# A graph network of four layers: gathers begun three places ahead instead of two, and the maximum's pieces at the front of a place

## The chip, the core and the metric

The kernel runs on one core of one Trainium2 chip. The metric is the time of the whole program on the device, in microseconds. The engines are PE (TensorE: matmuls and transposes), DVE (VectorE), ACT (ScalarE), POOL (GpSimd) and SP (SyncE, which here only issues DMAs); each runs its own instructions in order and waits for the others by semaphores.

## What is computed

Eight graphs (batches) of 2048 nodes with 256 features go through four layers; each layer adds its output to x. The adjacency is 0/1 and symmetric.

```python
h = relu(layernorm(x)); x = x + L0(adj, h)   # the first 25 neighbours' features, elementwise maximum
h = relu(layernorm(x)); x = x + L1(h, adj)   # attention, 4 heads of 64
h = relu(layernorm(x)); x = x + L2(h, adj)   # mean over the neighbours
h = relu(layernorm(x)); x = x + L3(h, adj)   # attention, one head of 256

# L0, for every node:
vals, idx = top_k(where(A != 0, -arange(N), -inf), 25)
agg = max over the 25 rows h[idx]            # rows that don't exist: -inf, or 0 where degree <= 25
out = relu(concatenate([h, agg]) @ W + b)
```

## The kernel before

A tile is 128 nodes; a batch has 16 tiles, the program 128. Layer 0 of batch b+1 is worked beside layers 1 to 3 of batch b, and that of batch 0 by itself at the start (the opening). Its work on one tile is cut in two halves. The **front** of a tile (`slot_front`) loads its adjacency rows, casts them on ACT, transposes them on PE, evacuates them on ACT (kept for the later layers in `adjT`), packs eight bits to a word on PE, and lets DVE find the first 25 neighbours; their numbers go to `idx`, which has two buffers. POOL then issues 25 indirect DMAs, each of which gathers one neighbour's row (256 f32) for the 128 nodes into `gath`, also two buffers of 25 rows. The **back** of a tile (`slot_back`) waits for the gather, takes the maximum of the 25 rows into `cat` (DVE), transposes the concatenation (PE), copies it (ACT), multiplies by W (PE) and adds to x (DVE).

A place (slot) is the back of tile T and the front of tile T + LAG, in 16 parts. `slot` calls each engine's work part by part: PE's transposes of the adjacency at parts 0 and 5 and its packing at 3 and 8; ACT's evacuations at 1, 2, 6, 7 and the copy of the adjacency word at 9 (L655); DVE's selection at 12 to 15 (it begins with `key`, L1120, and ends with `idx`, L1143); the concatenation's transposes at 10, ACT's copy at 11 (L677), the product at 12, DVE's addition at 15 (L1184). DVE's maximum is done in four pieces at the parts of `MAX_AT`. In the opening (`alone`) a piece is one reduction of a quarter of the columns (L1161); later the pieces are pairwise maxima of halves (L1152) and a last one into `cat` (L1178), which signals `reduced`.

`body` lays the parts of the places between the steps of the main work of a batch, evenly over a pair of steps' blocks. `PLAN` says how many places each phase takes: prep1 2, attend1 (four heads) 4, prep2 2, mean 3, prep3 1, attend3 (one head) 4. The first eight places of the opening, and one or two places in the phases prep1 to prep3, also carry `pre`, which normalises and stores the next batch's h in the table that the gathers read. Since every engine is in order, a part that waits holds up all the main work behind it on that engine.

POOL's work is `slot_front` alone, at part 15: it waits for `reduced.free(T, 2)`, that is for the maximum of tile T − 2, whose `gath` buffer it fills, and for `idx_ready`. `table_row`, `pre` and SP's loads of `cat` and `x1` stay as they are.

Of the kernel before, what the change touches and what calls it, by code (L numbers as in the profile page):

```python
# [48 lines left out]
S = 25  # L49
# [7 lines left out]
LAG = 2  # L57
# [47 lines left out]
def gnn_kernel(nc, x, adj, w0, b0, w1, a1s, a1d, w2m, w2u, b2, w3, a3, const, out):  # L105
    ctx = ExitStack()
    with ctx:
# [182 lines left out]
        MAX_AT = (0, 3, 6, 8)  # L290
# [6 lines left out]
        def body(eng, b, do, front=lambda s: True, pre=True, slots=True):  # L297
# [86 lines left out]
        def program(eng, do):  # L384
# [27 lines left out]
        class Part:  # L412
# [8 lines left out]
            def slot_back(self, T, par, n, part, front, alone): pass  # L421
# [17 lines left out]
            def slot(self, b, sh, par, part, front, k):  # L439

                known = isinstance(sh, int)
                alone = isinstance(b, int) and b < 0
                enters = not known or front(2 * sh + par)
                next_enters = not known or front(2 * sh + par + 1)
                Tf, Tb, n = front_tile(b, sh, par), back_tile(b, sh, par), half(b, sh)
                if part == 0:  # L450
                    self.slot_back(Tb, par, n, part, enters, alone)
                if enters:
                    self.slot_front(Tf, par, n + LAG // 2, part)
                if k is not None:
                    self.pre(16 * (b + 2) + 2 * k, 8 * (b + 2) + k, part)
                if part != 0:
                    self.slot_back(Tb, par, n, part, enters, alone)
                if next_enters:
                    self.ahead(Tf + 1, part)
# [24 lines left out]
        def _(sp):  # L484
            class Do(Part):
# [54 lines left out]
                def slot_back(self, T, par, n, part, front, alone):  # L540
# [64 lines left out]
        def _(act):  # L605
            class Do(Part):
# [66 lines left out]
                def slot_back(self, T, par, n, part, front, alone):  # L673
# [135 lines left out]
        def _(pe):  # L809
            class Do(Part):  # L810
# [41 lines left out]
                def slot_back(self, T, par, n, part, front, alone):  # L852
# [142 lines left out]
        def _(dve):  # L995
# [57 lines left out]
            class Do(Part):  # L1053
# [63 lines left out]
                def slot_front(self, T, par, n, part):  # L1117
# [32 lines left out]
                def slot_back(self, T, par, n, part, front, alone):  # L1150
# [5 lines left out]
                    if alone and part in MAX_AT:  # L1156
                        i = MAX_AT.index(part)
# [7 lines left out]
                    if part == MAX_AT[0]:  # L1165
                        halve(0, 12, 6)
                    if part == MAX_AT[1]:
                        halve(6, 18, 6)
                    if part == MAX_AT[2]:
# [3 lines left out]
                    if part == MAX_AT[3]:  # L1173
# [5 lines left out]
                    if part in MAX_AT:  # L1179
# [175 lines left out]
```

## Time and profile before

| | us |
|---|---|
| time before, median of 3 runs | 7518.04 (7516.22 to 7602.97) |
| the profiled execution's own time | 7535.86 |
| its span in the trace | 7534.0 |
| PE, DVE, ACT, POOL busy | 5252.3, 4670.5, 2088.6, 3479.3 |

The program has three stretches: the opening up to about 740 us, seven batches of some 900 us each with layer 0 of the next batch beside them, and the last batch from about 7000 us by itself. A row of the timeline gives the start and the length of an instruction, its line, the tiles out<-in, and in brackets how long its engine was idle before it and who released it; "remote" is a release for which the trace has no origin, "issue" a rest in which the engine waited for nothing that the trace shows. Matmuls are named by their accumulator.

### The profile page before, as it was taken

What the parts mean: (1) busy time and instruction counts of PE and PEld (TensorE: products, weight loads), DVE (VectorE), ACT (ScalarE), POOL (GpSimd) and SP (SyncE); (2) the same over time, 40 slices, a digit from 0 to 9 for tenths busy, and PEclk for the clock granted to TensorE, in tenths of its full rate; (3) what the DMA queues carried; (4) which work ended last, traced back from release to release, by engine and by line L of the source; (5) the groups of instructions that cost most, each with busy time, mean ns of one, the idle gap of its engine ahead of it and who ended that gap; (6) DMA issues with size and microseconds to landing.
All of it is one profiled execution on the core that took longest, in us unless ns stands there. A gap on an engine that the chain in (4) does not pass through costs nothing.

```text
span 7534.0 us, 85178 instructions
## 1 busy us (share of the span) xinstructions
PE 5252.3 (70%) x23860; PEld 3104.4 (41%) x23860; DVE 4670.5 (62%) x9897; ACT 2088.6 (28%) x4103; POOL 3479.3 (46%) x3204
## 2 busy tenths in 40 slices
PE   1212786778867696676866769667786669767999
PEld 1111334553345432463335533355334543356347
DVE  5544685457745587456865569546785458745653
ACT  2211323322233222323133131332323322231222
POOL 4656445454444544555444544446445454554000
PEclk8555897888878798887988889788898879878999
DMA  5434226442263423633245322544226442363021
GB/s 161 136 114 121 86 71 184 121 122 77 85 183 115 126 63 103 193 115 100 65 131 167 111 87 76 156 141 134 80 78 185 119 124 76 101 184 90 6 71 53
DMA packets 660564, 849.36 MB, mean 113 GB/s; under 512 B 80356, under 2 KB 491752, under 8 KB 659944
## 3 DMA queue, kind: packets, MB, share of 16 engines
q0 software_dynamic: 153600, 419.64, 19.2%
q10 hardware_dynamic: 344064, 268.50, 12.5%
q1 hardware_dynamic: 162408, 155.53, 6.5%
q8 instruction: 204, 3.34, 0.2%
q14 instruction: 288, 2.36, 0.1%
HBM read 774.13 MB, written 69.21 MB: 112 GB/s over the span
## 4 chain that ended last, share of the span: by engine, by line
PE 43%; another core or an unknown queue 19%; DVE 15%; issue 12%; ACT 5%; DMA 3%; ACTq 2%; DVEq 1%; SPq 0%
PE acc L951 17%; PE acc L957 8%; PE acc L897 4%; DVE edge L1264 4%; DVE top L1047 3%; DVE key L1050 2%; PE acc L987 2%; PE acc L989 2%; PE acc L988 2%; PE psH L864 2%; ACT hb L686 1%; DVE gath L1152 1%; PE psT L833 1%; PE psB L918 1%
## 5 line engine op out<-in xcount | busy, mean ns | idle before, releaser
L597 POOL DMA_INDIRECT gath<-htab,idx x3200 | 3479.1, 1087 | 3449.4 <-issue 1960.6
L951 PE MATMUL acc<-edge,region 128*65 128x512 f32 x4096 | 1861.3, 604 | 113.9 <-DVE edge L1264 86.6
L1264 DVE SCALAR_TENSOR_TENSOR edge<-region,gg,adjT 128x1024 f32<-128x1024 f32 (+1 forms) x1536 | 1640.8, 1107 | 351.5 <-ACT region L739 107.1
L957 PE MATMUL acc<-region,edge 128*128 128x257 f32 x4096 | 1018.6, 402 | 174.6 <-issue 92.7
L951 PEld LDWEIGHTS acc<-edge,region 128*65 128x65 f32 x4096 | 550.7, 140 | 1161.1 <-issue 1011.4
L957 PEld LDWEIGHTS acc<-region,edge 128*128 128x128 f32 x4096 | 804.8, 201 | 327.4 <-issue 167.1
L1152 DVE TENSOR_TENSOR gath<-gath 128x1536 f32<-128x1536 f32 (+2 forms) x672 | 782.6, 1178 | 55.0 <-issue 20.4
L639 ACT ACTIVATE adjT_b<-psT 128x1024 bf16<-128x1024 bf16 x256 | 262.7, 1026 | 1452.7 <-PE psT L833 689.6
L897 PE MATMUL acc<-w_s,edge 128*128 128x512 f32 (+2 forms) x1536 | 625.2, 554 | 3.8 <-issue 3.8
L1047 DVE MAX8 top<-key 128x8 f32<-128x256 f32 (+1 forms) x1024 | 407.3, 398 | 156.4 <-remote 48.2
L1120 DVE SCALAR_TENSOR_TENSOR key<-psO,cst 128x256 f32<-128x256 f32 x128 | 54.0, 422 | 722.8 <-ACT cst L655 603.4
L987 PE MATMUL acc<-region,col_b 128*128 128x257 bf16 x1024 | 297.0, 290 | 146.4 <-issue 79.7
L897 PEld LDWEIGHTS acc<-w_s,edge 128*128 128x128 f32 x1536 | 339.1, 236 | 138.7 <-issue 91.6
L1318 DVE TENSOR_SCALAR den<-acc 128x1 f32<-128x1 f32 x128 | 20.0, 156 | 587.5 <-remote 307.3
L987 PE MATMUL acc<-region,edge 128*128 128x257 bf16 x1024 | 299.3, 292 | 92.0 <-ACT edge L793 66.2
L864 PE MATMUL psH<-w_s,catT 128*128 128x256 f32 x1024 | 341.6, 491 | 0.0
L874 PE MATMUL psB<-cst,hb 128*128 128x128 f32 x768 | 150.2, 329 | 270.1 <-ACT hb L686 169.1
L833 PE MATMUL psT<-ident_bf,adj_b 128*128 128x128 bf16 x2048 | 203.1, 242 | 192.6 <-ACT adj_b L660 108.7
L988 PE MATMUL acc<-region,col_b 128*128 128x256 bf16 x1024 | 297.0, 290 | 36.2 <-issue 35.9
L989 PE MATMUL acc<-region,edge 128*128 128x256 bf16 x1024 | 299.2, 292 | 23.4 <-issue 23.0
L988 PE MATMUL acc<-region,edge 128*128 128x256 bf16 x1024 | 298.5, 291 | 22.4 <-issue 22.3
L989 PE MATMUL acc<-region,col_b 128*128 128x256 bf16 x1024 | 298.7, 292 | 20.8 <-issue 20.4
(130 smaller groups left out, 5897.3 us busy)
## 6 DMA issues: line engine op xcount, KB each, us to landing
adj_i<-in_adj ACTq DMA_DIRECT2D x512, 256.0 KB
hb<-in_adj ACTq DMA_DIRECT2D x256, 256.0 KB
col_i<-in_adj ACTq DMA_DIRECT2D x256, 256.0 KB
gath<-htab,idx POOLq DMA_INDIRECT x3200
cat<-htab SPq DMA_DIRECT2D x128, 128.0 KB
x<-in_x SPq DMA_DIRECT2D x128, 128.0 KB
x1d<-x SPq DMA_DIRECT2D x128, 128.0 KB
xr<-x1d SPq DMA_DIRECT2D x32, 512.0 KB
```

The lines of the kernel that those rows point to most:

```text
L597: pool.indirect_dma_start(out=gath[:, par, s, :], out_offset=None, in_=htab, in_offset=bass.IndirectOffsetOnAxis(ap=idx[:, par, s:s + 1], ...
L833: ins = pe.transpose(psT[:, 512 * k + P * j:512 * k + P * j + P], adj_b[:, k, P * j:P * j + P], ident_bf[:, :])
L864: ins = pe.matmul(o_mm, catT[:, k, :], w0_s[:, k, :], start=False, stop=(k == 3))
L897: ins = pe.matmul(bank[:, 0:width], hT[n % 2][:, i, c, :], w[:, c, :], start=(c == 0), stop=(c == 1 and p != 2), skip_group_check=True)
L951: ins = pe.matmul(acc[0:F + 1, 2 * h + half, :], V[1][:, J, (F + 1) * head:(F + 1) * (head + 1)], here[:, 512 * half:512 * half + 512], st ...
L957: ins = pe.matmul(acc[:, k, 0:C + 1], here[:, P * k:P * k + P], V[3][:, J, :], start=(J == 0), stop=(J == NT - 1), skip_group_check=True)
L987: pe.matmul(acc[:, k, 0:C + 1], w, split[:, t, 2 * C:3 * C + 1], start=(t == 0), stop=False, skip_group_check=True)
L988: pe.matmul(acc[:, k, 0:C], w, split[:, t, 0:C], start=False, stop=False, skip_group_check=True)
L989: ins = pe.matmul(acc[:, k, 0:C], w, split[:, t, C:2 * C], start=False, stop=(t == NT - 1), skip_group_check=True)
L1047: steps.of(dve.max(top[:, 8 * r:8 * r + 8], values))
L1152: steps.of(dve.tensor_tensor(gath[:, par, a:a + n, :], gath[:, par, a:a + n, :], gath[:, par, b:b + n, :], ALU.max))
L1264: dve.scalar_tensor_tensor(ring[p][:, n % EDGES[p], :], wB_of[p][:, h if p == 1 else q, :], gg[:, J, head:head + 1], adjT[:, J, bass.ds((( ...
```

## The change

LAG goes from 2 to 3. The front in a place is now that of tile T + 3; since 3 is odd it goes to the other `idx` and `gath` buffer than the tile whose back stands in the same place. The prologue ahead of the loop makes three fronts instead of two, and the last batch but one has one front fewer. The two-deep `gath` stays, so POOL's gather for tile T + 3 waits for the maximum of T + 1. As the indices of T + 3 overwrite those of T + 1, DVE waits for the gather of T + 1 before it writes them. The pieces of the maximum stand at parts 0, 1, 2, 3 in the opening and in all phases but attend1, where they stay at 0, 3, 6, 8.

```diff
-LAG = 2
+LAG = 3
...
-        MAX_AT = (0, 3, 6, 8)
+        MAX_AT = {True: (0, 3, 6, 8), False: (0, 1, 2, 3)}
...
                     k = pre_0 + i if pre and i < pres else None
-                    side += [lambda part=part, sh=sh, par=par, k=k: do.slot(b, sh, par, part, front, k) for part in range(PARTS)]
+                    apart = phase == "attend1"
+                    side += [lambda part=part, sh=sh, par=par, k=k: do.slot(b, sh, par, part, front, k, apart) for part in range(PARTS)]
...
             for T in range(LAG):
                 for part in range(PARTS):
-                    do.slot_front(T, T, 0, part)
+                    do.slot_front(T, T % 2, T // 2, part)
...
                 if enters:
-                    self.slot_front(Tf, par, n + LAG // 2, part)
+                    self.slot_front(Tf, (LAG + par) % 2, n + (LAG + par) // 2, part)
...
                     if part == 15:
                         first_bits(key[:, 0:S * WORD], 1, 4)
 
+                        if not isinstance(T, int) or T >= 2:
+                            dve.wait_ge(gathered[par], 16 * S * n)
                         dve.tensor_scalar(idx[:, par, :], top[:, 0:S], -1.0, cst[:, bass.ds(T + C_OFF, 1)], ALU.mult, ALU.add)\
...
+                    max_at = MAX_AT[apart]
...
-                    if part == MAX_AT[0]:
+                    if part == max_at[0]:
                         halve(0, 12, 6)
```

Three places in the order of the instructions, which shifts by one to four line numbers after the change.

POOL at the start of the program, up to its loop over the opening's places (`x24` is the rest of a tile's gathers). Before:

```order
L597 DMA gath<-htab,idx 128x256 [waits idx_ready,h_dma,reduced]
L597 DMA gath<-htab,idx 128x256 x24
L597 DMA gath<-htab,idx 128x256 [waits idx_ready,h_dma,reduced]
L597 DMA gath<-htab,idx 128x256 x24
L399 UNCONDITIONAL_BRANCH
L593 ISA [waits h_dma]
L597 DMA gath<-htab,idx 128x256 [waits reduced,idx_ready]
L597 DMA gath<-htab,idx 128x256 x24
L593 REGISTER_ALU [waits h_dma]
```

After:

```order
L598 DMA gath<-htab,idx 128x256 [waits idx_ready,h_dma,reduced]
L598 DMA gath<-htab,idx 128x256 x24
L598 DMA gath<-htab,idx 128x256 [waits idx_ready,h_dma,reduced]
L598 DMA gath<-htab,idx 128x256 x24
L598 DMA gath<-htab,idx 128x256 [waits idx_ready,h_dma,reduced]
L598 DMA gath<-htab,idx 128x256 x24
L400 UNCONDITIONAL_BRANCH
L594 ISA [waits h_dma]
L598 DMA gath<-htab,idx 128x256 [waits reduced,idx_ready]
```

A third tile's 25 gathers now stand ahead of the loop.

DVE in the opening, from the end of one place's selection to the next place's maximum. Before:

```order
L1047 MAX top<-key 128x8 [waits chain]
L1143 ISA [waits chain]
L1143 TENSOR_SCALAR idx<-top,cst 128x25
L1015 ISA [waits idx_ready,chain]
L1182 REGISTER_ALU
L1184 SCALAR_TENSOR_TENSOR x<-psH,x 128x256 [waits x1_ld,o_done]
L1161 TENSOR_REDUCE cat<-gath 128x64 [waits cat_tr,gathered1]
L1161 TENSOR_REDUCE cat<-gath 128x64 x3
```

After (`gathered1` is the buffer of the tile whose maximum follows):

```order
L1048 MAX top<-key 128x8 [waits chain]
L1145 ISA [waits chain]
L1146 ISA [waits gathered1]
L1146 TENSOR_SCALAR idx<-top,cst 128x25
L1016 ISA [waits idx_ready,chain]
L1186 REGISTER_ALU
L1188 SCALAR_TENSOR_TENSOR x<-psH,x 128x256 [waits x1_ld,o_done]
L1165 TENSOR_REDUCE cat<-gath 128x64 [waits cat_tr,gathered1]
L1165 TENSOR_REDUCE cat<-gath 128x64 x3
```

The wait for the gather now also stands ahead of the indices.

DVE in attend3, the second of its four places, from the third to the last piece of the maximum (L1264, after the change L1268, makes an attention edge). Before:

```order
L1152 TENSOR_TENSOR gath<-gath 128x1536
L1152 TENSOR_TENSOR gath<-gath 128x768 [waits chain]
L1015 ISA [waits chain]
L1261 REGISTER_ALU
L1264 REGISTER_ALU [waits mm3]
L1264 SCALAR_TENSOR_TENSOR edge<-region,gg,adjT 128x512
L1261 REGISTER_ALU
L1264 REGISTER_ALU [waits mm3]
L1264 SCALAR_TENSOR_TENSOR edge<-region,gg,adjT 128x512
L1152 TENSOR_TENSOR gath<-gath 128x256 x2
L1178 TENSOR_TENSOR cat<-gath 128x256 [waits cat_tr,chain]
L1015 ISA [waits chain]
```

After:

```order
L1155 TENSOR_TENSOR gath<-gath 128x1536
L1155 TENSOR_TENSOR gath<-gath 128x768 [waits chain]
L1016 ISA [waits chain]
L1265 REGISTER_ALU
L1268 REGISTER_ALU [waits mm3]
L1268 SCALAR_TENSOR_TENSOR edge<-region,gg,adjT 128x512
L1155 TENSOR_TENSOR gath<-gath 128x256 x2
L1182 TENSOR_TENSOR cat<-gath 128x256 [waits cat_tr,chain]
L1016 ISA [waits chain]
L1265 REGISTER_ALU
```

Between the third and the fourth piece there were two edges, now there is one.

## Rows read from the trace of the kernel before

**Rows 1.** The page: span, busy time of each engine, a group of instructions
```profile
span 7534.0 us, 85178 instructions
PE 5252.3 (70%) x23860; PEld 3104.4 (41%) x23860; DVE 4670.5 (62%) x9897; ACT 2088.6 (28%) x4103; POOL 3479.3 (46%) x3204
...
L1152 DVE TENSOR_TENSOR gath<-gath 128x1536 f32<-128x1536 f32 (+2 forms) x672 | 782.6, 1178 | 55.0 <-issue 20.4
```

**Rows 2.** The tile of the gathered rows: durations (ns), who waited for it (us, times)
```profile
L597 POOL DMA_INDIRECT gath<-htab,idx x3200: 941/949/2561, 43.7 to 6928.0; - x189
...
  DVE cat L1161: 36.9, 5
```

**Rows 3.** Stretches: opening; batch 5's attend1, mean, attend3; last batch's mean, attend3
```profile
core 0: us, PE busy (x) PEld busy (x) DVE busy (x) ACT busy (x) POOL busy (x), PEclk, DMA share, GB/s
77.00:722.00 645.00, 125.70 (x711) 85.79 (x711) 334.41 (x647) 115.94 (x172) 377.97 (x399) 0.57 0.42 122
5336.60:5601.10 264.50, 249.75 (x782) 90.43 (x783) 230.20 (x316) 58.78 (x134) 113.01 (x94) 0.98 0.23 68
5714.70:5883.90 169.20, 113.57 (x895) 86.80 (x896) 82.93 (x251) 62.81 (x103) 76.61 (x74) 0.82 0.69 203
5946.70:6127.00 180.30, 143.12 (x708) 117.01 (x709) 116.03 (x247) 36.69 (x61) 116.75 (x105) 0.90 0.43 126
7294.80:7385.40 90.60, 88.16 (x766) 75.87 (x767) 26.75 (x96) 41.64 (x67) 0.00 (x0) 0.94 0.72 207
7411.00:7528.40 117.40, 114.69 (x524) 99.21 (x524) 49.50 (x78) 7.12 (x17) 0.00 (x0) 0.98 0.04 14
```

**Rows 4.** Waits (engine line <- whom: us, times, longest): opening, then 740 to 7534
```profile
ACT adjT_b L639 <- remote: 376.4, 16, 34.8
...
DVE key L1120 <- ACT cst L655: 459.8, 31, 29.0
```

**Rows 5.** Timeline of the opening, POOL then ACT: start, us, what [idle before <-releaser]
```profile
121.30 0.95 POOL L597 DMA_INDIRECT gath<-htab,idx  x1 [14.95 <-issue]
...
353.36 0.95 POOL L597 DMA_INDIRECT gath<-htab,idx  x1 [7.70 <-issue]
...
392.01 0.94 POOL L597 DMA_INDIRECT gath<-htab,idx  x1 [7.63 <-issue]
...
474.73 0.95 POOL L597 DMA_INDIRECT gath<-htab,idx  x1 [20.43 <-issue]
...
388.65 1.02 ACT L639 ACTIVATE adjT_b<-psT 128x1024 bf16<-128x1024 bf16 x1 [18.47 <-remote]
...
434.29 1.02 ACT L639 ACTIVATE adjT_b<-psT 128x1024 bf16<-128x1024 bf16 x1 [28.29 <-remote]
...
462.32 1.02 ACT L639 ACTIVATE adjT_b<-psT 128x1024 bf16<-128x1024 bf16 x1 [25.05 <-remote]
```

**Rows 6.** Timeline of the opening, DVE
```profile
77.07 11.02 DVE L1161 TENSOR_REDUCE cat<-gath 128x64 f32<-128x1600 f32 x4 [14.43 <-DMA gath<-htab,idx]
...
367.99 0.42 DVE L1120 SCALAR_TENSOR_TENSOR key<-psO,cst 128x256 f32<-128x256 f32 x1
...
390.97 0.24 DVE L1143 TENSOR_SCALAR idx<-top,cst 128x25 uint32<-128x25 f32 x1 [0.16 <-DVE top L1047]
...
464.56 0.42 DVE L1120 SCALAR_TENSOR_TENSOR key<-psO,cst 128x256 f32<-128x256 f32 x1 [28.75 <-ACT cst L655]
...
473.69 0.24 DVE L1143 TENSOR_SCALAR idx<-top,cst 128x25 uint32<-128x25 f32 x1 [0.15 <-DVE top L1047]
```

**Rows 7.** Timeline of batch 0's mean phase: POOL, PE, ACT
```profile
1226.80 0.94 POOL L597 DMA_INDIRECT gath<-htab,idx  x1 [0.30 <-issue]
...
1218.34 0.26 PE L833 MATMUL psT<-ident_bf,adj_b 128*128 128x128 bf16 x1 [1.13 <-issue]
...
1231.28 1.02 ACT L639 ACTIVATE adjT_b<-psT 128x1024 bf16<-128x1024 bf16 x1 [16.46 <-remote]
```

**Rows 8.** Timeline of batch 3's attend3 phase: POOL, ACT
```profile
4341.51 0.95 POOL L597 DMA_INDIRECT gath<-htab,idx  x1 [51.42 <-DVE idx L1143]
...
4295.66 0.60 ACT L677 ACTIVATE catT<-psH 128x512 f32<-128x512 f32 x1 [50.85 <-remote]
```

More of the change, by code:

```diff
@@ L420, in slot_front, with slot_back @@
             def slot_front(self, T, par, n, part): pass
-            def slot_back(self, T, par, n, part, front, alone): pass
+            def slot_back(self, T, par, n, part, apart, alone): pass
             def prep_start(self, p, b): pass
@@ L437, in end, with slot @@
             def end(self, b): pass
-            def slot(self, b, sh, par, part, front, k):
+            def slot(self, b, sh, par, part, front, k, apart=False):
                 known = isinstance(sh, int)
@@ L450, in slot @@
                 if part == 0:
-                    self.slot_back(Tb, par, n, part, enters, alone)
+                    self.slot_back(Tb, par, n, part, apart, alone)
                 if enters:
-                    self.slot_front(Tf, par, n + LAG // 2, part)
+                    self.slot_front(Tf, (LAG + par) % 2, n + (LAG + par) // 2, part)
                 if k is not None:
@@ L456, in slot @@
                 if part != 0:
-                    self.slot_back(Tb, par, n, part, enters, alone)
+                    self.slot_back(Tb, par, n, part, apart, alone)
                 if next_enters:
@@ L538, in pre, with slot_back @@
                             sp.dma_start(htab[bass.ds(table_row(u + i), P), :], xa[:, i, :]).then_inc(h_dma, 16)
-                def slot_back(self, T, par, n, part, front, alone):
+                def slot_back(self, T, par, n, part, apart, alone):
                     if part == 0:
@@ L671, in ahead, with slot_back @@
                         self.cast(T, part - 14)
-                def slot_back(self, T, par, n, part, front, alone):
+                def slot_back(self, T, par, n, part, apart, alone):
                     if part == 11:
@@ L850, in slot_front, with slot_back @@
                         pack((3, 8).index(part))
-                def slot_back(self, T, par, n, part, front, alone):
+                def slot_back(self, T, par, n, part, apart, alone):
                     if part == 10:
@@ L1148, in slot_front, with slot_back @@
                         steps.end()
-                def slot_back(self, T, par, n, part, front, alone):
+                def slot_back(self, T, par, n, part, apart, alone):
                     def halve(a, b, n):
                         steps.of(dve.tensor_tensor(gath[:, par, a:a + n, :], gath[:, par, a:a + n, :], gath[:, par, b:b + n, :], ALU.max))
+                    max_at = MAX_AT[apart]
                     if part == 0:
                         dve.wait_ge(gathered[par], 16 * S * n + 16 * S)
-                    if alone and part in MAX_AT:
-                        i = MAX_AT.index(part)
+                    if alone and part in max_at:
+                        i = max_at.index(part)
                         if i == 0:
@@ L1164, in slot_back @@
                         return
-                    if part == MAX_AT[0]:
+                    if part == max_at[0]:
                         halve(0, 12, 6)
-                    if part == MAX_AT[1]:
+                    if part == max_at[1]:
                         halve(6, 18, 6)
-                    if part == MAX_AT[2]:
+                    if part == max_at[2]:
                         halve(0, 6, 6)
@@ L1172, in slot_back @@
                         halve(0, 3, 3)
-                    if part == MAX_AT[3]:
+                    if part == max_at[3]:
                         halve(0, 2, 1)
@@ L1178, in slot_back @@
                         dve.tensor_tensor(cat[:, C:2 * C], gath[:, par, 0, :], gath[:, par, 1, :], ALU.max).then_inc(reduced.sem, 1)
-                    if part in MAX_AT:
+                    if part in max_at:
                         steps.end()
```

## The prediction

> **What bounds the kernel now.** I read the page first, then the gather's tile, a table of stretches, the waits, and the timelines of the opening, of one mean phase and of the worst stall.
>
> No engine is full: PE is busy 5252 us of 7534, DVE 4671, POOL 3479 [rows 1]. The gathers are 3200 indirect DMAs, 25 for each of 128 tiles. Almost nobody waits for them: DVE waited 36.9 us in 5 places of the opening [rows 2], and all the idle time in front of the later maxima is 55.0 us [rows 1]. So a gather that lands earlier is worth at most 36.9 + 55.0 = 92 us by itself.
>
> What matters more is what happens beside a gather. In the opening (16 places, 77 to 722 us) PE works 126 us of 645 and DVE 334 [rows 3]; the greatest wait is ACT's for PE's transposes, 376.4 us in 16 pieces, which the trace puts down to nobody ("remote") [rows 4]. The timelines show its shape. A gather starts at 353.36 and ends 7.63 us before 392.01, at 384.38, so it takes 31.0 us. ACT's evacuation comes at 388.65, after 18.47 us of waiting that began some 17 us into that gather [rows 5]. DVE needs from 367.99 to 390.97, 23.0 us, for a chain of selections that takes 464.56 to 473.69, 9.1 us, while POOL rests [rows 6]. From 392.01 on two gathers stand back to back and end at 474.73 − 20.43 = 454.3; ACT waits 28.29 us and again 25.05 us, until 462.32, 8 us behind the last [rows 5]. In the mean phase a single gather does it: PE's transposes, a tenth of a microsecond apart by themselves, come with rests of 1.13 us, and ACT is let go at 1231.28, some 3.5 us after POOL's last issue of 1226.80 ended [rows 7]. So I read: the first 16 or so of a gather's 31 us cost the others nothing, the rest and 3 to 8 us behind it slow every engine's small instructions and signals (the loud end, below), and back-to-back gathers are the worst case. What causes it the trace doesn't tell. Long instructions don't mind it: four reductions keep their 11.0 us [rows 6].
>
> How much of that lies in the later batches: compare batch 5 with the last one, which has no places. Mean: PE busy 113.6 of 169.2, against 88.2 of 90.6. One-head attention (attend3): 143.1 of 180.3, against 114.7 of 117.4. PE idles 55.6 + 37.2 = 92.8 us in the two where the last batch idles 5.1; seven batches make 614 us that are neither PE's old nor its new work. The four-head attention leaves less: 249.8 of 264.5 [rows 3].
>
> **The change part by part.** *One more front ahead of the loop.* The prologue now selects tile 2 too. Part of it falls on DVE's 14.43 us of waiting for gather 0 [rows 6]; in exchange the last batch but one has one front fewer, and I set the rest equal to that. But gather 2, which now starts at 121.30 after 14.95 us of rest [rows 5], can follow gather 1 at once: −15 us.
>
> *The gather of tile T+3 waits for the maximum of T+1, no longer for a selection just finished.* Its indices are ready a place before, so it starts when the maximum at the front of the next place is done. In the opening the quiet first 16 us of a gather then cover the concatenation, the statistics and the fast selection; its loud end falls on the next 11.0 us of reduction, which don't mind. A place of the first eight takes 392.01 − 353.36 = 38.7 us [rows 5]: 11.0 of reduction, 23.0 of selection, 1 for the result, 3.7 left for the statistics. With the selection at 9.1 it would be 24.8, and POOL would bind at 25 × 1.25 = 31.3: up to 7.4 us each, 59 for eight. But with POOL bound its gathers stand back to back, the bad case, so I take under half: −25 us. The last eight take (645 − 8 × 38.7) / 8 = 41.9 us each. There I see a cycle of two gathers back to back, 62.6 us, and then a rest until the result and one reduction are through, 3 + 11 us: 77 for two, 38.5 each, 3.4 less, 27 for eight, of which I take −20 us.
>
> *The later batches.* A place is 40 to 80 us long (180.3 / 4 = 45 in the one-head attention [rows 3]) and a gather 31 and more of them, so POOL keeps up either way, and the same number of gathers falls in each phase. What moves is which parts of the place the loud end meets. Before, the gather starts with the place and its end meets parts 5 to 9, where PE and ACT hand the adjacency back and forth, with PE's attention matmuls queued behind on PE. After, it starts behind part 3 (part 8 in the four-head attention) and its end meets parts 10 to 15: three handovers (concatenation, copy, result) and DVE's selection. DVE's wait for the adjacency word, 459.8 us in 31 pieces behind the opening [rows 4], is the one that becomes shorter. It isn't all on the path, since in attention eight edge buffers lie between DVE and PE. Bounds: 0, and the whole 614 of PE's idle time. I take a tenth of the 460, −46 us, near zero because the gathers' number and length stay the same.
>
> *The maximum's pieces at parts 0 to 3 rather than 0, 3, 6, 8.* The same operations, 782.6 us for 112 tiles, 7.0 us each [rows 1], now nearly in one go. In the one-head attention eight edges lie in store, by the last batch 8 × 117.4 / 64 = 14.7 us of PE work [rows 3]: hidden; were it not, 7 us a place would cost 7 × 28 = 196. In the mean DVE owes only short finishes, each up to 7 us later with four accumulators: hidden. In the four-head attention, where DVE is busy 230 of 264 us [rows 3], nothing moves. 0 us.
>
> *The new wait ahead of the indices* asks for gather T+1 at part 15, just ahead of the wait that was there at part 0 of the next place. Queued behind it on DVE are the indices and the result's addition. It costs only where a place is shorter than POOL's 31.3 us: the opening, counted above. 0 us elsewhere.
>
> Sum: 7534 − 15 − 25 − 20 − 46 = 7428 for the profiled execution, whose own time of 7536 is 18 above the median of 7518. So **7410 us**.
>
> A rule bears on this. The Trainium skill, "DMA: Bandwidth & Descriptors", Rules for kernel authors, says to issue a DMA early, do other work, and wait for its semaphore late. By that rule alone the gain is at most what is waited for on gathers now, and the rows say that little is left of it; it would give 7426 on the median at best.
>
> **The rivals.** *The quiet start is worth more (7280).* If the opening comes near POOL's bound (645 down to 16 × 31.3 + 44 = 545, −100) and a fifth of the 614 is saved (−123), the sum with the −15 is 7534 − 238 = 7296, about 7280 on the median. For it: DVE's chain of 23.0 against 9.1 us [rows 6]. Against it: back-to-back gathers [rows 5].
>
> *Nothing changes (7510).* Gathers weren't waited for, their number is the same, and the loud end only meets other instructions. For it: PE crawls in the mean whatever stands in its queue [rows 7].
>
> *Slower (7620).* The result's chain meets the loud end. Now that is seen at one place: gathers without rest until 4341.51 − 51.42 = 4290.1, and ACT's copy of the concatenation waits 50.85 us until 4295.66, with PE and DVE's result behind it [rows 8]. After the change parts 10 to 12 always stand some 20 us into a gather. If each result must wait for the gather's end and 5 us more, a place can't be shorter than about 10 + 35 + 5 = 50 us; in the one-head attention it is 45 now, so 5 us times 28 places, 140 us, less the opening's 35: 7639, on the median about 7620. It decides from the point where gather end + 5 lies behind part 15.
>
> A further rule: the Trainium skill, "GPSIMD Engine Reference", section 8, says that GpSimd shares its SBUF interfaces with VectorE, with contention when VectorE reads two SBUF inputs. The trace agrees: one issue takes 378.0 / 399 = 0.95 us in the opening and 113.0 / 94 = 1.20 us in the four-head attention [rows 3]. It changes POOL's time only, which has rest to spare there.
>
> **How the numbers follow.** Forecast (7330 to 7480) 0.44, large gain 0.20, nothing 0.18, slower 0.18. The likeliest gives 7410. The range, 7280 to 7590, leaves out about half of the large gain and half of the slower case. Two per cent, about what can be told from no change, lies at 7368 and 7668: faster is the large gain and a quarter of the forecast, 0.31; slower is the part of its case in which more than the one-head attention pays, 0.13; the rest is 0.56.
>
> **What would show it.** In the profile after: gather 2 at about 107 us; the opening's places at 33 to 40 us; gathers starting 1 us behind the maximum, at the front of a place; ACT's nameless waits for transposes in the opening well below 376 us; DVE's wait for the adjacency word under 460. Wrong would be: mean or one-head attention longer than 170 and 180 us with ACT waiting for the concatenation until a gather ends, or more gathers back to back.

## The result, and the profile after

| | us |
|---|---|
| time after, median of 4 runs | 8379.53 (8366.68 to 8414.74) |
| time before, on the same chip, median of 4 runs | 7529.19 (7516.22 to 7602.97) |
| ratio | 1.111, 95% interval 1.103 to 1.120 |

The change makes the kernel 11% slower. I had forecast 7410 us and a range up to 7590; even the rival that ended on the slow side, 7620, is 760 us short. The page of the kernel after, with its most telling groups (busy us, mean ns | idle us of the engine just before them, and what ended it):

```profile
span 8412.9 us, 85400 instructions
...
PE 5272.2 (63%) x23860; PEld 3099.1 (37%) x23860; DVE 4670.1 (56%) x9897; ACT 2083.4 (25%) x4103; POOL 3161.8 (38%) x3204
...
L598 POOL DMA_INDIRECT gath<-htab,idx x3200 | 3161.6, 988 | 4606.5 <-DVE cat L1182 3344.1
...
L1155 DVE TENSOR_TENSOR gath<-gath 128x1536 f32<-128x1536 f32 (+2 forms) x672 | 781.9, 1177 | 45.8 <-issue 7.4
...
L1121 DVE SCALAR_TENSOR_TENSOR key<-psO,cst 128x256 f32<-128x256 f32 x128 | 54.0, 422 | 926.7 <-issue 546.1
```

The work is the same as in [rows 1]: PE 5272 busy us against 5252, DVE 4670 against 4671, and the maxima take 781.9 against 782.6. POOL is even 317 us less busy. The span is 879 us longer, nearly all of it waiting. POOL's idle time ahead of a gather is now put down to DVE's last piece of the maximum, 3344 us of it. The gathers, whose effect on the others was my whole argument, are now the ones who wait.

The stretches that answer to [rows 3] (opening; attend1, mean and attend3 of batch 5; the columns are those of [rows 3]):

```profile
core 0: us, PE busy (x) PEld busy (x) DVE busy (x) ACT busy (x) POOL busy (x), PEclk, DMA share, GB/s
77.00:818.00 741.00, 124.30 (x744) 84.84 (x744) 344.00 (x675) 121.68 (x181) 399.80 (x421) 0.57 0.38 111
6010.50:6290.50 280.00, 256.53 (x783) 91.99 (x783) 230.06 (x316) 59.28 (x135) 93.65 (x85) 0.95 0.20 59
6433.70:6632.80 199.10, 116.50 (x896) 90.45 (x897) 83.01 (x251) 62.10 (x103) 71.11 (x75) 0.77 0.59 173
6694.60:6917.40 222.80, 152.93 (x707) 121.05 (x708) 115.73 (x247) 36.62 (x60) 98.39 (x100) 0.81 0.33 99
```

The opening is 741 us against 645, attend1 280.0 against 264.5, mean 199.1 against 169.2, attend3 222.8 against 180.3, with the busy time of DVE and ACT unchanged. Everything that carries a place is longer, attend3 most; the last batch, which has none, takes 557 us against 556 before, from the first matmul of its main work to the last. PE's granted clock is lower (mean 0.834 before, 0.798 after, between its levels of 1.2 and 2.4 GHz), but all PE busy time has grown by 20 us only: the clock is no cause here.

**One place of attend3, before.** POOL's first issue of two gathers, then DVE, then ACT (start, us, [idle before <- releaser]):

```profile
1484.62 0.95 POOL L597 DMA_INDIRECT gath<-htab,idx  x1 [16.33 <-issue]
...
1534.57 1.48 POOL L597 DMA_INDIRECT gath<-htab,idx  x1 [14.59 <-issue]
...
1485.38 1.75 DVE L1152 TENSOR_TENSOR gath<-gath 128x1536 f32<-128x1536 f32 x1
...
1499.74 0.42 DVE L1178 TENSOR_TENSOR cat<-gath 128x256 f32<-128x256 f32 x1
...
1521.94 0.42 DVE L1120 SCALAR_TENSOR_TENSOR key<-psO,cst 128x256 f32<-128x256 f32 x1 [19.06 <-issue]
...
1533.53 0.24 DVE L1143 TENSOR_SCALAR idx<-top,cst 128x25 uint32<-128x25 f32 x1 [0.15 <-DVE top L1047]
1534.14 0.42 DVE L1184 SCALAR_TENSOR_TENSOR x<-psH,x 128x256 f32<-128x256 f32 x1 [0.36 <-DVEq L1010]
...
1521.52 0.38 ACT L655 ACTIVATE cst<-psO 128x256 f32<-128x256 f32 x1 [18.45 <-remote]
```

The gather starts at 1484.62 and its last issue ends 14.59 us before 1534.57, at 1519.98: 35.4 us. The whole maximum, 1485.38 to 1500.16, lies beside its first half. Then DVE waits 19.06 us for the adjacency word, which ACT copies at 1521.52, 1.5 us behind the gather. Behind that stand only the selection (to 1533.77) and the next gather's start. Place: 35.4 + 14.6 = 50 us.

**One place of attend3, after:**

```profile
1640.31 1.31 POOL L598 DMA_INDIRECT gath<-htab,idx  x1 [25.84 <-DVE cat L1182]
...
1695.48 1.31 POOL L598 DMA_INDIRECT gath<-htab,idx  x1 [23.39 <-DVE cat L1182]
...
1639.06 0.42 DVE L1182 TENSOR_TENSOR cat<-gath 128x256 f32<-128x256 f32 x1
...
1666.39 0.42 DVE L1121 SCALAR_TENSOR_TENSOR key<-psO,cst 128x256 f32<-128x256 f32 x1 [20.94 <-issue]
...
1678.35 0.24 DVE L1146 TENSOR_SCALAR idx<-top,cst 128x25 uint32<-128x25 f32 x1 [0.15 <-DVE top L1048]
1682.06 0.42 DVE L1188 SCALAR_TENSOR_TENSOR x<-psH,x 128x256 f32<-128x256 f32 x1 [3.48 <-PE psH L865]
...
1683.25 1.75 DVE L1155 TENSOR_TENSOR gath<-gath 128x1536 f32<-128x1536 f32 x1
...
1694.22 0.42 DVE L1182 TENSOR_TENSOR cat<-gath 128x256 f32<-128x256 f32 x1
...
1665.97 0.38 ACT L656 ACTIVATE cst<-psO 128x256 f32<-128x256 f32 x1 [13.77 <-remote]
...
1676.04 0.60 ACT L678 ACTIVATE catT<-psH 128x512 f32<-128x512 f32 x1 [8.89 <-remote]
```

The gather runs from 1640.31 to 1695.48 − 23.39 = 1672.09, 31.8 us, and nothing large lies beside it: DVE waits 20.94 us ahead of the key, ACT 13.77 ahead of the word and 8.89 ahead of the concatenation. The result comes at 1682.06, 10 us behind the gather, and only then does the next maximum run, 1683.25 to 1694.64, and the next gather starts behind its last piece. Place: 31.8 + 11.2 + 12.2 = 55.2 us. The gather that starts there had its indices since 1678.59, and the rows that this maximum reads had been issued by 1640.31 − 25.84 = 1614.47. It isn't data that is late. The maximum has moved from beside the gather to between two gathers.

Over all gathers of the seven attend3 phases (25 of each kernel; worked out from the trace; a gather is counted to the end of its last issue): before, a gather 34.4 us and 11.8 us from its end to the next one, 46.2 in all; after, 31.9 + 25.3 = 57.2. In the mean phases 33.6 + 24.4 = 58.0 before, 31.1 + 36.3 = 67.4 after. That POOL needs 317 us less is the same fact: an issue is slower beside DVE's maximum, and none is beside it now.

**The opening, after:**

```profile
124.44 0.95 POOL L598 DMA_INDIRECT gath<-htab,idx  x1 [21.86 <-DVE cat L1165]
...
401.16 0.95 POOL L598 DMA_INDIRECT gath<-htab,idx  x1 [29.88 <-DVE cat L1165]
...
493.21 0.95 POOL L598 DMA_INDIRECT gath<-htab,idx  x1 [29.72 <-DVE cat L1165]
...
101.10 0.42 DVE L1121 SCALAR_TENSOR_TENSOR key<-psO,cst 128x256 f32<-128x256 f32 x1 [42.18 <-issue]
...
112.56 11.09 DVE L1165 TENSOR_REDUCE cat<-gath 128x64 f32<-128x1600 f32 x4 [0.54 <-DVEq L1011]
...
415.32 11.01 DVE L1165 TENSOR_REDUCE cat<-gath 128x64 f32<-128x1600 f32 x4
...
471.01 0.42 DVE L1121 SCALAR_TENSOR_TENSOR key<-psO,cst 128x256 f32<-128x256 f32 x1 [27.49 <-ACT cst L656]
...
481.35 11.03 DVE L1165 TENSOR_REDUCE cat<-gath 128x64 f32<-128x1600 f32 x4
...
454.57 1.02 ACT L640 ACTIVATE adjT_b<-psT 128x1024 bf16<-128x1024 bf16 x1 [41.86 <-remote]
```

Two gathers from 401.16 stand back to back until 493.21 − 29.72 = 463.49; ACT waits 41.86 us in them for transposes, DVE gets its key at 471.01, and then come selection, result and maximum in a row before POOL may go on: 493.21 − 401.16 = 92.05 us for two places. And the first maximum is taken at 112.56, not at 77.07 [rows 6], since DVE stands 42.18 us at the key of the third front.

### The profile page after: what moved, and what is told of

Read it like the earlier page. It is cut to its first block, busy times and chain, and to the rows that moved or that the text cites. A ratio compares the mean times of both kernels' runs of the same rounds, so it can differ in the third digit from the quotient of the medians.

```text
span 8412.9 us, 85400 instructions
## 1 busy us (share of the span) xinstructions
PE 5272.2 (63%) x23860; PEld 3099.1 (37%) x23860; DVE 4670.1 (56%) x9897; ACT 2083.4 (25%) x4103; POOL 3161.8 (38%) x3204
## 3 DMA queue, kind: packets, MB, share of 16 engines
q10 hardware_dynamic: 344064, 268.50, 11.2%
## 4 chain that ended last, share of the span: by engine, by line
PE 36%; another core or an unknown queue 23%; issue 17%; DVE 15%; ACT 5%; DMA 2%; ACTq 2%; DVEq 1%; SPq 0%
PE acc L952 12%; PE acc L958 6%; DVE edge L1268 5%; PE acc L898 4%; DVE gath L1155 3%; PE acc L988 3%; PE acc L990 2%; PE acc L989 2%; DVE top L1048 2%; DVE key L1051 2%; PE psH L865 1%; DMA col_i<-in_adj 1%; PE psB L919 1%; PE psB L875 1%
## 5 line engine op out<-in xcount | busy, mean ns | idle before, releaser
L598 POOL DMA_INDIRECT gath<-htab,idx x3200 | 3161.6, 988 | 4606.5 <-DVE cat L1182 3344.1
L952 PE MATMUL acc<-edge,region 128*65 128x512 f32 x4096 | 1882.9, 609 | 136.2 <-DVE edge L1268 70.5
L1268 DVE SCALAR_TENSOR_TENSOR edge<-region,gg,adjT 128x1024 f32<-128x1024 f32 (+1 forms) x1536 | 1635.5, 1104 | 457.1 <-ACT region L740 154.5
L958 PE MATMUL acc<-region,edge 128*128 128x257 f32 x4096 | 1067.4, 411 | 343.8 <-issue 251.3
L958 PEld LDWEIGHTS acc<-region,edge 128*128 128x128 f32 x4096 | 821.9, 205 | 525.5 <-issue 328.6
L1155 DVE TENSOR_TENSOR gath<-gath 128x1536 f32<-128x1536 f32 (+2 forms) x672 | 781.9, 1177 | 45.8 <-issue 7.4
L898 PE MATMUL acc<-w_s,edge 128*128 128x512 f32 (+2 forms) x1536 | 580.7, 520 | 109.3 <-ACT edge L694 109.2
L898 PEld LDWEIGHTS acc<-w_s,edge 128*128 128x128 f32 x1536 | 312.8, 218 | 233.8 <-ACT edge L694 110.6
L844 PE MATMUL psO<-pack_bf,adjT_b 128*128 128x32 bf16 x2048 | 105.3, 180 | 468.2 <-issue 360.1
L863 PE MATMUL psH<-bias 3*128 3x256 bf16 x128 | 42.3, 331 | 464.4 <-ACT catT L678 306.7
```

What stands on the lines that cost most here:

```text
L598: pool.indirect_dma_start(out=gath[:, par, s, :], out_offset=None, in_=htab, in_offset=bass.IndirectOffsetOnAxis(ap=idx[:, par, s:s + 1], ...
L898: ins = pe.matmul(bank[:, 0:width], hT[n % 2][:, i, c, :], w[:, c, :], start=(c == 0), stop=(c == 1 and p != 2), skip_group_check=True)
L952: ins = pe.matmul(acc[0:F + 1, 2 * h + half, :], V[1][:, J, (F + 1) * head:(F + 1) * (head + 1)], here[:, 512 * half:512 * half + 512], st ...
L958: ins = pe.matmul(acc[:, k, 0:C + 1], here[:, P * k:P * k + P], V[3][:, J, :], start=(J == 0), stop=(J == NT - 1), skip_group_check=True)
L1268: dve.scalar_tensor_tensor(ring[p][:, n % EDGES[p], :], wB_of[p][:, h if p == 1 else q, :], gg[:, J, head:head + 1], adjT[:, J, bass.ds((( ...
```

## The experiments

**Which half of the change is it?** The pieces at the front alone, and the three places alone.

```diff
-LAG = 3                          # lag2_front_max; and without the wait ahead of the indices
+LAG = 2
```
```diff
-        MAX_AT = {True: (0, 3, 6, 8), False: (0, 1, 2, 3)}        # lag3_old_max
+        MAX_AT = {True: (0, 3, 6, 8), False: (0, 3, 6, 8)}
```

> Only the pieces of the maximum move to parts 0 to 3 outside attend1; gathers stay two places ahead. Theory L (the loop): in the changed kernel a gather can start only behind the maximum of the next place, that maximum stands on DVE behind the last place's result, and the result is held until the running gather has ended, so a place costs gather + result + maximum in a row. With LAG 2 a gather starts on its indices, so nothing of that arises: 7450 to 7600 us. Rival B (the burst): four pieces in a row hold up DVE's edges and finishes, 7 us in 96 later places and more: 8000 us or more.

Measured: 7613 us, ratio 1.013 (1.009 to 1.017): 13 us above the range of theory L, far from B's 8000.

> LAG 3 with the pieces at parts 0, 3, 6, 8 everywhere. Theory L: the gather starts later in its place still, so it is as slow as the changed kernel or slower, 8400 to 9200 us. Rival B: the loss is undone, 7500 to 7600 us.

Measured: 8411 us, ratio 1.119 (1.113 to 1.124): as L has it, and B falls. The pieces cost 1.3% by themselves, mostly in attend3 (a phase has 196 us against 184), where I had set 0 us. The rest is the three places; with them, the old positions of the pieces inside a place make nothing better.

**Is it the order, or just POOL's wait?** The kernel before with one digit changed: a gather waits for the maximum of the tile ahead of its own, as it does with three places and two buffers.

```diff
-                    pool.wait_ge(reduced.sem, reduced.free(T, 2))
+                    pool.wait_ge(reduced.sem, reduced.free(T, 1))
```

> The kernel before, but POOL waits for the maximum of tile T-1 instead of T-2 ahead of the gather of T, so that the gather starts behind the next place's maximum as in the changed kernel; LAG, indices and the order on every other engine are as before. Theory L: gather and maximum come one after the other and the gather must land within its own place: 8400 us or more. Rival D (the third tile in flight and the new wait ahead of the indices are what costs): about 7530, at most 7700 us.

Measured: 8443 us, ratio 1.123 (1.117 to 1.128).

```profile
L597 POOL DMA_INDIRECT gath<-htab,idx x3200 | 3142.7, 982 | 4699.9 <-DVE cat L1178 3327.0 <-issue 1120.7 <-DVE cat L1161 208.9
...
L1152 DVE TENSOR_TENSOR gath<-gath 128x1536 f32<-128x1536 f32 (+2 forms) x672 | 781.5, 1177 | 275.8 <-DMA gath<-htab,idx 222.4 <-DVEq L1010 15.4 <-issue 11.4
...
DVE cat L1161 <- DMA gath<-htab,idx: 284.2, 14, 23.9
```

Nearly the same loss and the same signature (4700 us of idle POOL, 3327 of it for DVE's last piece) with LAG, selection and result as before; theory L holds, D falls. The match of the totals is in part chance, since a gather must now land within its own place: DVE waits 222 us for rows behind the opening and 284 in it, which the changed kernel does not. The clean part is the mean and attend3 phases, where hardly any rows are waited for (19 us in all): they take 195.5 and 216.8 us on average of the seven batches, against 197.2 and 221.0 after the change and 172.0 and 184.5 before, and in attend3 a gather of 31.5 us is followed by 25.2. There the loss sits in one relation: a gather that may start only behind the maximum that DVE takes next.

**Does the late result hold the maximum?** After the change DVE's result stands between the gather's end and the maximum. Moved earlier, outside attend1, it should let the maximum go sooner.

```diff
-                    if part == 10:      # PE, concatenation; ACT's copy 11 -> 5, product 12 -> 6, DVE's result 15 -> 10
+                    if part == (10 if apart else 4):
```

> The changed kernel with the result outside attend1 moved ahead: the concatenation's transposes at part 4, its copy at 5, the product at 6, DVE's addition at 10, that is into the first 16 us of the gather that the maximum releases. Theory L, with the result as the step that is held: the result comes before the gather's loud end and the next maximum stands only behind the selection, 7700 to 8200 us. If it is the selection (the adjacency word) that is held as long as the result, no change: 8300 to 8450. Rival B: no change.

Measured: 8785 us, ratio 1.168 (1.162 to 1.174): slower still, and outside all three expectations.

```profile
L1188 DVE SCALAR_TENSOR_TENSOR x<-psH,x 128x256 f32<-128x256 f32 x128 | 54.3, 424 | 634.3 <-remote 469.6 <-PE psH L865 75.9 <-issue 75.5
L1121 DVE SCALAR_TENSOR_TENSOR key<-psO,cst 128x256 f32<-128x256 f32 x128 | 53.8, 421 | 1004.1 <-ACT cst L656 765.6 <-issue 231.7 <-DVEq L1011 6.3
```

DVE's idle time ahead of the key went from 927 to 1004 us and ahead of the result from 217 to 634. The key now starts 4 us behind the gather's end (median of the places from tile 20 on; after the change 17 us ahead of it, with the result 8 us behind it), and the whole selection stands between it and the maximum. In attend3 a gather of 31.6 us is followed by 30.4 us, against 25.3. Moving one handover earlier doesn't free the path; it decides which one is held, and how much is queued behind it.

**Does it go if the maximum is taken out of the loop?** With three places DVE can take tile T+1's maximum in the place of T, ahead of the selection, so that the gather starts behind the indices again.

```diff
-        MAX_AT = {True: (0, 3, 6, 8), False: (0, 1, 2, 3)}
+        MAX_AT = {True: (2, 5, 8, 11), False: (8, 9, 10, 11)}
...
+                    T, n, par = T + 1, n + par, 1 - par     # in DVE's slot_back, for the maximum only
```

> LAG 3 as in the changed kernel, but DVE takes the maximum of tile T+1 at parts 8 to 11 of place T (2, 5, 8, 11 in attend1), ahead of that place's selection and result, so that the gather of T+3 can start as soon as its indices are written; tile 0's maximum stands ahead of the loop. Theory L: with the maximum out of the way between one gather and the next the loss is gone, 7400 to 7650 us, though LAG is 3, three fronts stand ahead and the new wait is there. Rival D (the third tile in flight, the other buffer, the new wait): stays above 8200.

Measured: 7966 us, ratio 1.064 (1.058 to 1.071), between the two theories. attend3 is back at 185 us a phase (35.0 + 13.2 a gather), but the mean phase has 188 and the opening is still 85 us longer than before. DVE now waited 576 us ahead of the last piece, and 235 more ahead of the opening's reductions; both overwrite the concatenation that PE transposes at part 10: a wait the experiment had brought along. Two more kernels were to take it away: result at parts 4 to 7 (lag3_ahead_early), and the pieces besides at 0, 3, 6, 8 outside the opening (lag3_ahead_front).

> Three places ahead, the maximum of tile T+1 taken in the place of T at parts 8 to 11 as in the run before with that change (7965 us), and now also the result of T earlier in every place: PE's transposes of the concatenation at part 4, ACT's copy at 5, the product at 6, DVE's addition at 7. In that earlier run DVE waited 576 us ahead of the last piece of the maximum, which overwrites the concatenation that PE transposes only at part 10; the two lie side by side. Theory W (that wait, which the experiment itself put in, is the rest of the loss): with the transposes at part 4 it goes, the mean phase returns from 187 to some 172 us, and the time to 7450 to 7650. Theory C (the maximum has to lie beside the first part of a gather for the gather to be cheap; pieces at parts 8 to 11 stand behind it): the mean phase stays above 182 us and the time at 7800 to 8000.

Measured: 8759 us, ratio 1.151 (1.145 to 1.157).

> As the other kernel of this pair, with the pieces of tile T+1's maximum at parts 0, 3, 6, 8 of the place of T in every phase but the opening (there at 8 to 11). The gather of T+3 still begins behind the indices at the end of the place, and the maximum lies beside its first part, as in the kernel before. Theory W: as fast as the other one within 1%, 7450 to 7650. Theory C: this one is 7400 to 7600 while the other stays at 7800 or more. If both are above 7800 with the opening at 90 us more than before, neither holds, and a gather that starts two places ahead of its maximum costs by itself.

Measured: 7856 us, ratio 1.031 (1.025 to 1.036). Neither expectation fits. W falls for the first kernel: it is slower, not faster. C had the sign right for the pair and both numbers too low. The last clause asks for an opening 90 us longer than before; it is 39 and 43 us longer, so whether a gather that starts two places ahead costs by itself isn't settled. The first kernel's rows in attend3 say why:

```profile
1597.58 0.94 POOL L598 DMA_INDIRECT gath<-htab,idx  x1 [39.15 <-DVE idx L1151]
...
1665.35 0.94 POOL L598 DMA_INDIRECT gath<-htab,idx  x1 [36.38 <-DVE idx L1151]
...
1640.79 0.42 DVE L1198 SCALAR_TENSOR_TENSOR x<-psH,x 128x256 f32<-128x256 f32 x1 [35.69 <-PE psH L865]
...
1641.79 1.75 DVE L1160 TENSOR_TENSOR gath<-gath 128x1536 f32<-128x1536 f32 x1
...
1651.71 0.42 DVE L1191 TENSOR_TENSOR cat<-gath 128x256 f32<-128x256 f32 x1
...
1664.32 0.24 DVE L1151 TENSOR_SCALAR idx<-top,cst 128x25 uint32<-128x25 f32 x1 [0.16 <-DVE top L1048]
```

The gather ends at 1665.35 − 36.38 = 1628.97. DVE stood 35.69 us at the result, until 1640.79, and behind it in its queue were the whole maximum and the whole selection: 67.8 us a place. With the pieces ahead of the result they lie beside the gather, and the same program takes 903 us less. Over all of attend3 it is 31.3 + 33.9 against 34.8 + 14.3.

**The rule by itself.** The versions so far suggested one rule: in a place some handover to DVE isn't through until the gather is about over, so what DVE has in front of it is covered and what it has behind it, up to the next gather's start, is paid. That gives a number in advance, for the kernel before: 8.8 us more work on DVE per place, ahead of the wait or behind it. The edit is against the changed kernel set back to LAG 2, the old pieces and no wait ahead of the indices.

```diff
+                    if part == 4 and not apart and not alone:      # lag2_work_front; lag2_work_back: part == 14
+                        for again in range(5):
+                            halve(6, 18, 6)
+                            steps.wait()
+                        steps.end()
```

> The kernel before (two places ahead, pieces at 0, 3, 6, 8) with added work on DVE in 84 of its 128 places, those of all phases but the opening and the four-head attention: the second step of the maximum, whose result doesn't change when it is repeated, is done five times more, here at part 4 of the place, beside the first part of the gather and ahead of every handover that DVE waits for in the place. The step takes 1.76 us, so 5 x 1.76 = 8.8 us a place and 739 us of DVE in all. Theory H (from the seven versions measured so far: beside a running gather DVE's first wait for another engine lasts until the gather is over, so a place lasts the gather's 31 to 36 us and what DVE still has to do behind that wait; work ahead of the wait is covered): within 1.5% of before, 7500 to 7630. Theory G (DVE's work costs the same wherever it stands): 7850 to 8260, the same as its pair within 1.5%.

Measured: 7628 us, ratio 0.994 (0.991 to 0.998).

> The same added 8.8 us of DVE work in the same 84 places, now at part 14, between the selection that DVE had to wait for and the indices with which the next gather begins. Theory H: all of it is paid, 84 x 8.8 = 739 us, so 8150 to 8350, a ratio of about 1.09 to 1.11. Theory G: the same as its pair. A time under 7900 would say that a place has slack behind the held wait, and H would fall.

Measured: 8086 us, ratio 1.053 (1.046 to 1.060).

```profile
L598 POOL DMA_INDIRECT gath<-htab,idx x3200 | 3721.6, 1163 | 3296.9 <-issue 1887.3 <-DVE idx L1146 1366.5 <-SPq L523 40.1
...
L1155 DVE TENSOR_TENSOR gath<-gath 128x1536 f32<-128x1536 f32 (+2 forms) x1092 | 1521.1, 1401 | 80.4 <-issue 18.7 <-DVEq L1011 10.3 <-DVE gath L1155 5.9
...
5779.30:5938.00 158.70, 113.34 (x895) 89.85 (x896) 110.45 (x267) 63.01 (x103) 89.35 (x76) 0.85 0.74 219
6002.00:6203.10 201.10, 155.09 (x707) 125.25 (x708) 151.06 (x267) 36.70 (x61) 127.87 (x103) 0.86 0.37 111
```

```profile
L598 POOL DMA_INDIRECT gath<-htab,idx x3200 | 3490.6, 1091 | 3999.0 <-issue 2507.0 <-DVE idx L1146 1450.4 <-SPq L523 40.3
...
L1155 DVE TENSOR_TENSOR gath<-gath 128x1536 f32<-128x1536 f32 (+2 forms) x1092 | 1521.9, 1402 | 101.2 <-issue 23.5 <-DVE key L1051 20.3 <-DVEq L1011 9.1
...
6150.40:6330.40 180.00, 120.03 (x896) 90.81 (x897) 103.18 (x252) 62.17 (x103) 76.88 (x73) 0.78 0.64 192
6403.90:6619.60 215.70, 159.24 (x707) 124.17 (x708) 151.28 (x267) 36.62 (x60) 114.45 (x100) 0.81 0.34 102
```

Both kernels do the same 1521 us of halving, 739 more than before. At the front the total doesn't rise, as H has it, but this nothing is a sum of unlike parts: against the trace of the kernel before, which was taken on another chip, the mean phase is 17 us shorter (155 against 172) and attend3 13 us longer (198 against 184, 38.0 + 10.3 a gather). The gather is longer (1163 ns an issue against 1087 in the kernel before), and in the mean the rest behind it is shorter (37.1 + 17.2 against 33.6 + 24.4); why it shrinks that much no run shows. At the back the work costs 458 us more than in its pair, 62% of the 739, and less than H's range of 8150 to 8350: in attend3 35.1 + 18.6 a gather, 6.8 us more rest than before's 11.8 for 8.8 us of work, in the mean phase only 8 us in all for three places. And attend1, which has none of the added work, takes 281 us against 265. Theory G falls; H holds in its sign, for the total, and as an upper bound.

**Is it the gathers at all, and what of them?** The first 12 of 25 gathers only (the maximum then runs over 12 gathered rows and 13 of zeros), in both kernels; and all 25 with 64 of 256 columns, a quarter of the bytes (the other columns of the rows stay zero).

```diff
-                    for s in range(S):
+                    for s in range(12):
```
```diff
-                            out=gath[:, par, s, :], out_offset=None, in_=htab,
+                            out=gath[:, par, s, 0:64], out_offset=None, in_=htab,
```

> The kernel before with 12 of the 25 gathers per tile; the maximum still runs over 25 rows, 13 of them zeros or old, so the values of layer 0 are others and all other work is the same. If a gather has a loud end only from about 16 us on, a gather of 15 us has none: 6700 to 7000 us. If the slow stretches are not the gathers' doing: 7450 to 7550.

Measured: 6247 us, ratio 0.834 (0.828 to 0.839), below the 6700 to 7000 expected.

> The changed kernel with 12 of 25 gathers per tile, the same part left out. Theory L: a place still has gather and maximum in a row but the gather is 15 us and holds nobody, so the places are bounded by other work and the distance to the kernel before with 12 gathers falls from 850 us to under 200. If the loss is in the order on DVE or in LAG 3 itself it stays near 850.

Measured: 6585 us, ratio 0.879 (0.873 to 0.884).

> The kernel before with all 25 indirect DMAs per tile, but each row's first 64 of 256 columns only, a quarter of the bytes (the other columns hold zeros, so layer 0's values are others). If the slow stretches come from the bytes in flight: as with 12 gathers, 6700 to 7100 us. If from the number of DMAs, their descriptors or their completion signals: 7400 to 7550.

Measured: 7526 us, ratio 0.999 (0.994 to 1.004). In the kernel before, 12 gathers give back 7510 − 6247 = 1263 us, far more than the 92 us that anybody waits for rows, and a quarter of the bytes gives nothing. So it is the number of indirect DMAs that holds up the others, or something that goes with it, such as the number of rows or POOL's time issuing them, which no run varied by itself. (Part of the gain is PE's clock, 0.899 against 0.834 granted: PE is busy 5019 us instead of 5252.) The distance between the two orders shrinks from 850 to 338 us, not below 200 as expected. The traces show what remains: in attend3 18.4 + 17.3 = 35.7 us before and 15.5 + 27.9 = 43.4 after. After the change the maximum no longer lies beside the gather, and its 10 us between two gathers don't depend on the gather's length.

## Why the prediction was wrong

**The bound.** That hardly anybody waits for the rows, and that the others lose their time beside a gather, was right (12 gathers, narrow rows). The conclusion that all that moves is "which parts of the place the loud end meets" was the mistake. The signs named for being wrong came: the mean and attend3 phases of batch 5 took 199 and 223 us.

**Gather 2 at 107 us, −15.** It came at 124.44 [rows 5: 121.30]. I let part of the third front fall into DVE's 14.43 us of waiting, but its transposes and its word fell beside gathers 0 and 1, back to back, and DVE stood at its key until 101.10, with the first maximum behind it, at 112.56: 35 us later than before.

**The opening's places, −25 and −20.** I had 31.3 to 38.5 us a place; the first eight take 92.05 / 2 = 46.0. The cycle of two gathers I had seen, 62.6 us and a rest. But I put the rest at 14 us, result and one reduction, and it is 29.7: the selection had been held beside the gathers as well, and its 9 us stand in that rest too. The opening lost 96 us (741 against 645) instead of winning 60. One sign I had named did come, ACT's nameless waits for transposes in the opening fell from 376 to 295 us, and it was no gain.

**The later batches, −46.** The step that failed is the sentence "What moves is which parts of the place the loud end meets". Before, the 7 us of maximum and the edges between its pieces (14.8 us together in the place above) were what the gather's first half covered; I had even written that the first 16 us cost nothing. I moved the gather's start behind that work and looked only at what its end would meet. The sign I had named for it came true by name only: behind the opening DVE's waits at its key for ACT are 257 us, under 460. But its nameless waits there ("issue") rose from 111 to 376, so that DVE stands 634 us at the key where it stood 571, and over the whole run 927 against 723, with 217 against 141 at the result. The result and the maximum now stand between the gather's end and the next gather. For the 112 places behind the opening the loss is 879 − 96 = 783 us, 7.0 each, where the sum had a gain of 46.

**The pieces at the front, 0 us.** With two places, 1.3%. With three it makes no difference clear of noise (ratios 1.119 and 1.111, whose intervals overlap).

**The wait ahead of the indices, 0 us outside the opening.** Right, as far as the runs show: after the change DVE rests 49 us in all ahead of the indices, none of it for rows, and the loss is there without that wait (lag2_pool_waits).

**The slow rival, 7620.** It had the mechanism nearly whole: a place can't be shorter than the maximum, the gather and what is behind it, 10 + 35 + 5 = 50 us, with attend3 at 45. Measured are 12.2 + 31.8 + 11.2 = 55.2 in the place above, 57.2 over all: behind the gather it isn't 5 us for one handover but some 11, for the rest of the selection and the result. And I priced it in attend3 alone, 28 of 112 places, as if a phase whose places are longer than 50 us had slack. The mean phase has places of 58 us and lost 9 us on each: its rest is also a chain that starts anew when the gather ends. With the measured 11.0 a place in attend3, 28 × 11.0 = 308 us (by the lengths of the phases, 221.0 against 184.5, it is 7 × 36.5 = 256); the other phases and the opening make the larger part. Its chance, 0.18, was too small: it needed only that one order, gather behind maximum, puts in a row two things that had lain side by side, and the order of instructions showed that plainly.

**The rule on early issue.** "DMA: Bandwidth & Descriptors", Rules for kernel authors, in the Trainium skill says: "Issue the DMA early, do compute, wait on its semaphore late". The change does so: behind the opening a maximum now starts 73 us (median; 42 to 115) behind the last issue of its gather, and the kernel is 11% slower. So the trace of this case disagrees with it as a rule for time. With two buffers, earlier relative to the use also meant later relative to the buffer's release.

**Left open.** What in the chip holds signals and small instructions beside indirect DMAs: many of the releases are "remote" or "issue" in the traces, and no run looked inside. How much of the mean phase's loss with the maximum ahead comes from the wait for the concatenation also stays open, since each kernel that removed it held another step. The best version with three places is still 3% slower than the kernel before, and no run splits that up: DVE rests 981 us ahead of the result in it.

## What to carry to other kernels

Before a transfer is started earlier or later, list per engine what lies beside it and what lies between its end and the next one's start; if the other engines crawl beside it, the loop is its length and what stands behind the handovers it holds, and independent long work belongs beside it. A buffer's release is the real start of a gather: a deeper lead with the same two buffers ties the start to a later consumer, so count the new loop (release, transfer, tail, consumer) before counting what the lead hides. When a handover is moved out of the way, ask which one is held instead and what is queued behind that.

## What the runs showed of the chip

- The cost of the indirect DMAs to the others goes with their number (or what goes with it), not with their bytes: 25 narrow ones 0.999, 12 wide ones 0.834.
- 739 us of added DVE work beside them left the total where it was (0.994), though it makes each issue slower: 988 ns on average with nothing of the maximum beside, 1087 with it, 1163 with more. Shorter issues on POOL (317 busy us fewer) went with 11% more time.
- I had read that the first 16 us of a gather are quiet. With 12 gathers, 14.7 us of issues, DVE's result still comes 14.6 us behind the last issue in the changed kernel (median from tile 20 on; 8.4 with 25), and 22.8 in the kernel before (15.4 with 25). That fits handovers that are a chain with a length of its own, of which a gather slows a part; whether the first 16 us are quiet no run shows by itself.
